# Sixteen tiles instead of eight written out in one turn of the engines' loops, in the stage of six transformer layers

## The reference

```python
x = x + _layernorm(_L0_attn_ref(_layernorm(x), ...))
x = x + _layernorm(_L0_ffn_ref(_layernorm(x), ...))

# _L0_ffn_ref: DEPTH = 6, HEADS = 16, DIM_HEAD = 64, WINDOW = 32
for i in range(DEPTH):
    x = attn_layer(shift_tokens(x), Wqkv[i], q_scale[i], k_scale[i], Wo[i]) + x
    x = ffn_layer(shift_tokens(x), ln_g[i], ln_b[i], W1[i], b1[i], W2[i], b2[i]) + x

def attn_layer(x, Wqkv, qs, ksc, Wo):
    qkv = x @ Wqkv                       # 128 -> 3 * 1024
    q, k = l2norm(q) * qs, l2norm(k) * ksc
    q, k = rotary(q), rotary(k)
    return local_attention(q, k, v) @ Wo # windows of 32, each sees itself and the one before

def ffn_layer(x, g, bln, W1, b1, W2, b2):
    xn = layernorm(x) * g + bln
    a, gate = jnp.split(xn @ W1 + b1, 2, -1)
    return a * jax.nn.gelu(gate, approximate=False) @ W2 + b2
```

## Time and profile before

| | |
|---|---|
| median of 3 runs | 4550.41 us (4549.1 to 4551.08) |
| the profiled execution | 4545.86 us |
| its span, first to last instruction | 4544.1 us |
| mean granted TensorE clock | 0.967 of full speed |
| TensorE busy | 4209.9 us, 93% of the span |
| VectorE busy | 3701.0 us, 81% |
| ScalarE busy | 3584.1 us, 79% |
| GpSimd busy | 2338.2 us, 51% |
| mean DMA traffic | 79 GB/s |

### The profile page before, as it was taken

One profiled execution on the slowest core, in us unless ns is written; L12 is line 12 of the kernel. 1 busy time (PEld: TensorE's weight loads), 2 busy tenths in 40 slices (PEclk: granted clock), 3 DMA queues, 4 the chain that ended last, 5 costly groups with the idle time before them and its releaser, 6 DMA issues. The chain is left out here.

```text
span 4544.1 us, 138566 instructions
## 1 busy us (share of the span) xinstructions
PE 4209.9 (93%) x44000; PEld 2967.1 (65%) x44000; DVE 3701.0 (81%) x8420; ACT 3584.1 (79%) x6842; POOL 2338.2 (51%) x2840
## 2 busy tenths in 40 slices
PE   4899999966999999999999999999999999999994
PEld 2466666644766767767776677767777766776673
DVE  6688888876888888888888888888888888888884
ACT  1799999935888888888888888888888888888883
POOL 1000000016666666666666666666666666666671
PEclk7899999978999999999999999999999999999997
DMA  6677777712111111111111111111111111111111
GB/s 221 216 231 231 231 231 231 231 55 73 33 44 42 41 45 32 41 45 41 45 32 41 45 41 42 35 41 46 41 39 38 41 46 41 36 41 41 45 41 48
DMA packets 258908, 361.00 MB, mean 79 GB/s; under 512 B 44404, under 2 KB 216156, under 8 KB 257884
## 3 DMA queue, kind: packets, MB, share of 16 engines
q1 hardware_dynamic: 258140, 351.55, 25.7%
HBM read 151.19 MB, written 93.34 MB: 54 GB/s over the span
## 5 line engine op out<-in xcount | busy, mean ns | idle before, releaser
L1367 PE MATMUL la_ps<-la_Wqkv,la_xsT 128*128 (+1 forms) x2304 | 1201.1, 617 | 8.5 <-DVE la_rsk L1081 5.3
L1024 POOL TENSOR_TENSOR la_rt<-la_rt,la_rn 128x1024 f32<-128x1024 f32 x384 | 722.4, 1902 | 27.5
L1081 DVE TENSOR_TENSOR la_rsq<-la_ps,la_tab 128x1024 f32<-128x1024 f32 x384 | 469.7, 1223 | 140.9 <-ACT la_sq L1225 138.3
L1225 ACT ACTIVATE la_sq<-la_ps 128x512 f32<-128x512 f32 x768 | 453.7, 596 | 152.3 <-issue 62.0
L1088 DVE TENSOR_REDUCE la_ssum<-la_sq 128x8 f32<-128x512 f32 x768 | 502.6, 674 | 51.4 <-issue 51.4
L1402 PEld LDWEIGHTS la_ps<-la_kT,la_qB 128*64 128x64 f32 x12288 | 391.8, 138 | 146.7 <-issue 145.8
L1367 PEld LDWEIGHTS la_ps<-la_Wqkv,la_xsT 128*128 128x128 f32 x2304 | 378.6, 191 | 158.5 <-issue 121.3
L1081 DVE TENSOR_TENSOR la_rsk<-la_ps,la_tab 128x1024 f32<-128x1024 f32 x384 | 465.8, 1213 | 4.1 <-ACT la_sq L1225 3.9
L1433 PEld LDWEIGHTS la_ps<-la_Wo,la_oT 128*128 128x128 f32 x3072 | 365.1, 192 | 133.2 <-issue 132.3
L1402 PE MATMUL la_ps<-la_kT,la_qB 128*64 128x64 f32 x12288 | 435.1, 224 | 0.0
L122 POOL TENSOR_TENSOR la_ln_stats<-la_ln_stats,la_ln_power 128x1 f32<-128x1 f32 x192 | 105.4, 549 | 615.0 <-DVE la_ln_stats L117 615.0
(11 more groups left out here) (168 smaller groups left out, 10272.1 us busy)
## 6 DMA issues: line engine op xcount, KB each, us to landing
at_band<-skew_scratch SPq DMA_DIRECT2D x64, 1536.0 KB, 7.3
la_vs<-la_v SPq DMA_DIRECT2D x192, 384.0 KB, 3.5
skew_scratch<-at_R SPq DMA_DIRECT2D x64, 1024.0 KB, 6.7
la_vs<-la_v SPq DMA_DIRECT2D x192, 128.0 KB, 3.4
la_Wqkv<-in_wqkv SPq DMA_DIRECT2D x28, 384.0 KB, 3.6
kt_scratch<-pr_k SPq DMA_DIRECT2D x24, 384.0 KB, 3.2
qt_scratch<-pr_q SPq DMA_DIRECT2D x24, 384.0 KB, 4.0
at_qh<-qt_scratch SPq DMA_DIRECT2D x64, 144.0 KB
```

The lines of the kernel that those rows point to most:

```text
L1024: e.tensor_tensor(heads(rt, w), heads(rt, w), wide(rn[:, w * H:(w + 1) * H], D), ALU.mult)\
L1081: e.tensor_tensor(dst.rearrange("p f (h d) -> p f h d", d=D), ps[:, c % 2, :].rearrange("p (h d) -> p h d", d=D).unsqueeze(1).to_broadcast ...
L1225: e.activation(sq[:, c % 2, :], ps[:, c % 2, :], ACT.Square).then_inc(sq_ev.sem, 1)
L1367: e.matmul(ps[:, c % 2, :], xsT[:, m * P:(m + 1) * P], Wqkv[:, ds(layer(n) % 2, 1), c * 512:(c + 1) * 512], start=True, stop=True)\
```

## The change

`rounds` gets a fifth number, `unit`: how many places one turn of the hardware loop holds. The ring (how buffers go round) stays at 8 in the layers, and `unit` is 16. The first 8 tiles are written out as before. The loop now has 11 turns of 16 places, tiles 8 to 183, and the last 8 tiles (184 to 191) are written out ahead of the 7 places in which the work runs dry. Every engine, SyncE and GpSimd too, gets the longer body. In the other stages `unit` is the ring, as before; there only the way in which the tile's number is formed differs (`turn * unit + (ring + place)`, with turns counted from 0).

```diff
-def rounds(e, body, count, ring, deepest):
-
+def rounds(e, body, count, ring, deepest, unit=None):
+
+    unit = unit or ring
+    whole = (count - ring) // unit
     for g in range(ring):
         body(Turn(g, g, count, ring))
-    with e.Fori(1, count // ring) as turn:
-        for place in range(ring):
-            body(Turn(turn * ring + place, place, count, ring))
-    for g in range(count, count + deepest):
+    with e.Fori(0, whole) as turn:
+        for place in range(unit):
+            body(Turn(turn * unit + (ring + place), place % ring, count, ring))
+    for g in range(ring + whole * unit, count + deepest):
         body(Turn(g, g % ring, count, ring))
...
-            rounds(e, body, TILES, TB, DEEPEST)
+            rounds(e, body, TILES, TB, DEEPEST, 2 * TB)
```

## The result

| | before | after |
|---|---|---|
| median, measured side by side | 4549.76 us (4 runs, 4548.23 to 4551.08) | 4479.68 us (4 runs, 4478.64 to 4481.66) |
| the profiled execution | 4545.86 us | 4480.28 us |
| its span | 4544.1 us | 4478.4 us |
| mean granted TensorE clock | 0.967 | 0.968 |

The ratio is 0.9847, with a 95% interval of 0.9834 to 0.9861: 1.5% faster. The change takes 70 us off the median and 66 us off the profiled execution.

The account below looks back on a forecast made before the run. TensorE was taken as the bound inside a turn, with idle holes at back edges. Removing 12 at 4.6 us saves 55 us, all else 0: 4545.9 - 55 = 4491, as median 4550.4 - 55 = 4495 us; range 4486 to 4511 us.

Parts of the forecast that it names:

- the crossings in straight code and the loop's exit: Of 12 removed back edges, 11 become straight code and one the loop's exit; both were to cost nothing.
- the price of a removed back edge: Layers' loop: eight tiles with a back edge against eight without, 4.5 us, raised to 4.6; 12 x 4.6 = 55 us gained.
- of one that is left: The 10 back edges that stay in the layers' loop were to keep their price of 4.6 us.
- the 0 for register arithmetic: Register instructions per tile hide below TensorE's queued matmuls: 0 in the sum, at most 3 us either way.
- the 4.5 us between profile and median: Median before lies 4.5 us above the profiled execution; added to 4491 to give 4495 us.
- the main term: Removing 12 of 22 back edges in the layers' loop saves 55 us, within bounds of 28 to 61 us.
- Neither stretch: Two readings without a back edge: tiles 7 to 15, 137.8 us; six steps inside a later turn, 137.9 for eight.
- The makeup of the price: Back edge's 4.5 us: TensorE's pause 2.4, clock loss 1.6, and 0.5 from VectorE's pause as short waits.
- the 1.6 us for the clock: Granted clock of 0.91 over 18 us behind a back edge was to lose TensorE 1.6 us.
- GpSimd's longer body: Rival: the ten back edges left get dearer, GpSimd's above all, 1 to 2.8 us each, 4505 to 4523 us; 9%.
- The clock did not fall: Rival: without pauses to rest TensorE its granted clock falls over long stretches; at 0.97, 4586 us and slower; 3%.
- its lower end: 4486 us; the dearest back edge taken was 5.1 us, ScalarE's 2.8 and TensorE's 2.3 in full, 61 us for 12.

Follow-up runs that it names:

- The shift experiments: ScalarE's loop moved by idle waits: kernel before by 32 instructions, 4538.3 us, by 64, 4544.08 us; changed kernel by 32, 4489.46 us.

## Why the prediction was wrong

The direction and the count held: 22 pauses became 10 on TensorE, VectorE and ScalarE, the crossings in straight code and the loop's exit cost nothing, and the granted clock dips behind back edges that are left only. What failed is the sum, in four terms that all erred the same way: the price of a removed back edge (4.6 us, measured 4.9), of one that is left (4.6, measured 4.4), the 0 for register arithmetic (2.5 us) and the 4.5 us between profile and median (gone after the change). Together they make the 15 us. The makeup of the main term was wrong too. By the traces, the 66 us between the two profiled executions are 12 x 4.9 = 59 for the back edges removed, 10 x 0.5 = 5 for those left, and 2.5 for the eight tiles written out. (The layers also start 2 us earlier in the second trace, and 2 us are lost again behind the last tile's start.)

- **"So a back edge costs 142.3 - 137.8 = 4.5 us"**, raised to 4.6. This term was mis-sized; it is 4.9 (4.8 against the middle of the later turns). Neither stretch was a fair measure of eight tiles without a back edge: the first holds a tile of the start at 17.0 us that later takes 16.6, and the second was stretched from six steps to eight with a long one, of 18.0 us, at its head. That long step is not the back edge's alone: at the same place in the middle of the changed kernel's turn it takes 17.7 to 18.3 us. 12 x 0.3 = 4 us.
- **"It keeps 10 back edges, whose price I leave at 4.6 us."** The argument was only that a longer body could not make them dearer. They became cheaper, 4.4 instead of 4.9, for a reason that I had not thought of: the place of ScalarE's loop in its stream. 5 us. The shift experiments show that the place sets ScalarE's pause, and that eight tiles get 0.6 us shorter with it.
- **Register arithmetic, "0 in the sum".** On TensorE it does hide, as the kernel with TensorE alone written out shows. But the cost was looked for on the bound engine only, and writing out VectorE or ScalarE shortens the tiles, so what goes away with the loop there stands in the chain that TensorE waits for. 2.5 us here; over all tiles it would be 57 us, more than this change's forecast.
- **"The median of the runs shown is 4.5 us above that execution."** Carried over to the changed kernel, this added 4.5 us that were not there: after the change profile and median agree within 0.6 us.
- **The makeup of the price**, "2.4 + 1.6 = 4.0, and the 0.5 that is left is VectorE's pause", gave a number near the right one, by luck, from a sum that does not exist. Taking TensorE's pause away alone gives nothing or less. And the 1.6 us for the clock was read at one back edge and given to all. Over the 18 us behind each of the 22, the granted clock is 0.91 or 0.92 at 11 and 1.00 at the other 11. One of these, ahead of tile 56:

```profile
1985.00:2003.00 18.00, 16.86 (x191) 11.81 (x192) 13.79 (x28) 12.86 (x26) 11.09 (x13) 1.00 0.15 44
```

For the four tile steps that begin with the one ahead of the jump, the kernel before takes 73.65 us on average where the clock dips and 73.62 where it does not; in the changed kernel, where it dips behind 5 of 10, 73.01 and 72.93. So no more than 0.1 us goes with the dip in these two kernels. More can go with it in others: where nothing but TensorE pauses, it is 72.2 us in 18 cases with it against 71.3 in 4 without. The 4.9 us lie in the tile ahead of the jump, 20.4 us on average instead of 17.7 inside a turn, and in the one behind it, 18.6 instead of 16.6. Why pauses of 2.3 to 2.8 us make twice as much of the period is shown only so far as that they act on each other; the rest stays open.

Of the rivals, GpSimd's longer body costs nothing that shows: its root still waits for VectorE in all 180 cases, 4.3 us at most, and with GpSimd and SyncE written out the time of the one execution is within 0.1% of before. The clock did not fall in any long stretch, not even over three milliseconds at 99.9% busy. The range failed because its lower end was the dearest sum of pauses at an unchanged place, with nothing for what written-out code saves beside them.

## What to carry to other kernels

In this kernel a hardware loop's back edge stopped each of the three busiest engines for 2 to 3 us, and the work's period grew by 3.9 to 6.2 us whichever of them paused. It is worth removing on all engines at once: all written out gave 166 us. On one engine alone it gave less, 50 us on VectorE, half of it by faster tiles, and 23 on ScalarE (one execution each), and it cost time on TensorE, the bound. Price it from the period of work with and without a jump, taking the stretch without from two places far from any jump, and do not add up the engines' idle times. Code that a loop needs and written-out code does not costs time on the engines that the bound one waits for, even where it hides on the bound one; write the whole loop out if the program's size allows it. And do not put a price on a dip of the clock from one place: compare the places with it and without it.

## What was not expected of the hardware

The pause at a back edge depends on where the loop stands in an engine's instruction stream: ScalarE's was 2.8 us, and 2.1 us with the same loop 32 or 64 instructions further on, and in the longer loop it went from 2.15 to 2.7 us with a shift of 32. Removing the pauses from TensorE alone made the kernel slower, by 0.36% (0.23 to 0.48). In the kernel before, the granted clock fell behind 11 of the 22 back edges, after pauses of TensorE of 2.05 to 2.75 us, and stayed at 1.00 behind the other 11, after pauses of 2.04 to 2.58; the time across them was the same, 73.65 and 73.62 us. And a program of 192 tiles without a loop ran with no pause of issue over 1 us ahead of any first step: TensorE was 99.9% busy over 2968 us at full granted clock.
